# Attention block on one core: the small bias loads on SyncE's queue, the bias product behind the turning of the weight, and waits and orders around the images moved

## The reference

```python
residual = hidden_states                      # x: (16, 512, 32, 32) f32
h = group_norm(hidden_states, norm_gamma, norm_beta)   # 32 groups
q = conv1x1(h, wq, bq); k = conv1x1(h, wk, bk); v = conv1x1(h, wv, bv)
qf, kf, vf = (a.reshape(16, 512, 1024) for a in (q, k, v))
attn = softmax(einsum('bci,bcj->bij', qf, kf) * 512 ** -0.5, axis=2)
out = einsum('bcj,bij->bci', vf, attn).reshape(16, 512, 32, 32)
return residual + conv1x1(out, wo, bo)
```

## Time and profile before

| what | value |
|---|---|
| three runs | 2030.28, 2030.69, 2032.45 us, median 2030.69 |
| the profiled execution | 2031.8 us, its span in the trace 2029.9 us |
| instructions | 29828 |
| busy: PE, DVE, ACT, POOL | 98%, 80%, 49%, 16% of the span |
| mean granted clock of TensorE | 0.997 |
| HBM | 142 GB/s over the span |

### The profile page before, as it was taken

How to read it: one execution, slowest core, us unless ns; L and a number is a source line. 1 busy time by engine, 2 the same in 40 slices (tenths; PEclk the granted TensorE clock), 3 DMA queues, 4 the chain that set the end, 5 groups by cost and what they waited for, 6 DMA issues and landing times.

```text
span 2029.9 us, 29828 instructions
## 1 busy us (share of the span) xinstructions
PE 1985.6 (98%) x9924; PEld 1678.9 (83%) x9924; DVE 1630.4 (80%) x2284; ACT 999.5 (49%) x1529; POOL 325.8 (16%) x241
## 2 busy tenths in 40 slices
PE   9999999999999999999999999999999999999998
PEld 7787878878788787887878878787887878878887
DVE  7897787978879688696887969778797887978856
ACT  6464453645536464453644536445364553646443
POOL 2012120111202012020221201212011120201202
PEclk9999999999999999999999999999999999999999
DMA  6436152363424535154350533615236242363402
GB/s 238 150 146 162 60 163 93 145 165 124 102 84 151 159 145 124 42 176 134 145 155 31 174 116 145 159 74 150 93 145 165 98 119 93 146 164 145 86 28 42
DMA packets 55467, 255.45 MB, mean 126 GB/s; under 512 B 8208, under 2 KB 8208, under 8 KB 50832
## 3 DMA queue, kind: packets, MB, share of 16 engines
q1 hardware_dynamic: 34896, 221.53, 28.7%
q0 software_dynamic: 18432, 33.56, 11.1%
q10 hardware_dynamic: 2112, 0.01, 0.1%
HBM read 214.18 MB, written 74.45 MB: 142 GB/s over the span
## 4 chain that ended last, share of the span: by engine, by line
PE 81%; DVE 7%; DMA 7%; issue 3%; ACT 2%; POOL 0%; DVEq 0%; SPq 0%; POOLq 0%; ACTq 0%
PE psum L406 27%; PE psum L407 27%; PE psum L408 27%; DMA out<-scores 6%; DVE h_lo L955 3%; DVE scores L1186 1%; ACT scores L749 1%; DVE scores L1028 1%; DVE wide L1179 0%; DVE red L1174 0%; ACT scores L704 0%; DVE big_lo L1053 0%; DMA scores<-in_wq 0%; DVE bn L886 0%; DVE big_lo L1139 0%
## 5 line engine op out<-in xcount | busy, mean ns | idle before, releaser
L406 PE MATMUL psum<-big_hi 128*128 128x512 f32 x1056 | 411.9, 390 | 2.8 <-POOL big_lo L348 2.8
L407 PE MATMUL psum<-big_lo,big_hi 128*128 128x512 f32 x1056 | 411.9, 390 | 0.0
L408 PE MATMUL psum<-big_hi,big_lo 128*128 128x512 f32 x1056 | 411.5, 390 | 0.0
L406 PE MATMUL psum<-big_hi,h_hi 128*128 128x512 f32 x896 | 350.7, 391 | 3.9 <-ACT room L815 3.2
L407 PE MATMUL psum<-big_lo,h_hi 128*128 128x512 f32 x896 | 349.4, 390 | 0.0
L408 PE MATMUL psum<-big_hi,h_lo 128*128 128x512 f32 x896 | 349.3, 390 | 0.0
L1118 DVE TENSOR_TENSOR scores<-psum,room 128x512 f32<-128x512 f32 x192 | 130.7, 689 | 185.3 <-ACT room L815 135.3
L408 PE MATMUL psum<-w_split,h_lo 128*128 128x256 f32 x896 | 253.6, 283 | 0.0
L407 PE MATMUL psum<-w_split,h_hi 128*128 128x256 f32 x896 | 253.6, 283 | 0.0
L406 PE MATMUL psum<-w_split,h_hi 128*128 128x256 f32 x896 | 253.5, 283 | 0.0
L815 ACT COPY room<-psum 128x512 f32<-128x512 f32 x192 | 112.8, 587 | 275.5 <-PE psum L408 275.5
(11 more groups left out here) (133 smaller groups left out, 3448.2 us busy)
## 6 DMA issues: line engine op xcount, KB each, us to landing
w_split<-kept_t SPq DMA_DIRECT2D x15, 3584.0 KB, 11.8
w_split<-kept_v SPq DMA_DIRECT2D x15, 3584.0 KB, 11.3
room<-in_x SPq DMA_DIRECT2D x64, 512.0 KB, 3.4
out<-scores POOLq DMA_DIRECT2D x128, 256.0 KB, 6.8
room<-in_x SPq DMA_DIRECT2D x60, 256.0 KB, 4.7
red<-in_x SPq DMA_DIRECT2D x30, 256.0 KB, 4.6
wide<-in_x SPq DMA_DIRECT2D x30, 256.0 KB, 8.3
kept_t<-w_split SPq DMA_DIRECT2D x1, 3584.0 KB, 11.0
```

The costliest lines, as they stand in the source:

```text
L406: nc.tensor.matmul(o, a_hi, b_hi, start=start, stop=False, skip_group_check=True)
L407: nc.tensor.matmul(o, a_hi, b_lo, start=False, stop=False, skip_group_check=True)
L408: return nc.tensor.matmul(o, a_lo, b_hi, start=False, stop=stop, skip_group_check=True)
```

## The change

- The loads of bq, gamma, beta and bo go from ACT's queue to SP's: bq behind wk and wq and ahead of x, the other three behind wo and ahead of wv.
- On PE the four products with the bias (`bias_summed`) go behind the turning of wo; the copy of the result (`t_bias`) on ACT goes behind the first part of wv, and PE waits for it before the product of wo and wv.
- wo is no longer loaded again: the product of wo's rows with bv (`row_dots`) is made by DVE in `make_first_t` from the first copy of wo; bv's load comes early.
- In image 0 `high_wv(3..6)` and `low_wv(3..6)` go behind the first pair of scores, and the six pieces of statistics behind that pair's last sums.
- At each turn of images, DVE makes D3 of row 0 (`begin_t`) ahead of outputs 4 to 7, and waits for one store at a time (`left`), only ahead of the sum that overwrites it; ACT makes snap "b" and the high part of D3 ahead of the bias of outputs 4 to 6.
- In the last image the last output block gets its bias and x on DVE and is stored by a plain DMA of SP.

```diff
@@ scratch rows, semaphores
+        rest = room[:, 7, :]
-        wo_again = [scores[:, n, :] for n in (2, 3, 10, 11)]
-        bv_rows, wo_bv_terms = scores[:, 6, :], scores[:, 7, :]
+        bv_rows, wo_bv_terms = scores[:, 13, :], scores[:, 12, :]
...
@@ SyncE
                 sp.dma_start(wq_raw[:, o, :], w_d["q"][:, o, :]).then_inc(wq_in[o], 16)
+            sp.dma_start(bq_s[:], bq_d, allow_slow_non_contiguous=True).then_inc(bq_in, 16)
             for k in (2, 3, 0, 1):
                 sp.dma_start(full[:, k, :], x_d[0][:, k, :]).then_inc(x0_in[k], 16)
             for o in range(KC):
                 sp.dma_start(wo_raw[:, o, :], w_d["o"][:, o, :]).then_inc(wo_in[o], 16)
+            for n, a in enumerate(vec_d):
+                sp.dma_start(vecs[:, n, :], a, allow_slow_non_contiguous=True).then_inc(vec_in, 16)
             for o in range(KC):
                 sp.dma_start(wv_raw[:, o, :], w_d["v"][:, o, :]).then_inc(wv_in[o], 16)
+            sp.wait_ge(wv_split, KC)
+            sp.dma_start(bv_rows, bv.partition_broadcast(P)).then_inc(bv_in, 16)
...
-                    for c in range(KC):
-                        sp.dma_start(wo_again[c], w_d["o"][:, c, :]).then_inc(wo_back, 16)
-                    sp.dma_start(bv_rows, bv.partition_broadcast(P)).then_inc(bv_in, 16)
...
+                else:
+                    sp.wait_ge(h_split, count(b, 7, 7))
+                    sp.dma_start(rest, x_d[b][:, KC - 1, HALF:N]).then_inc(rest_held, 16)
+                    sp.wait_ge(rest_in, count(b, 16, 16))
+                    sp.wait_ge(last_added, 1)
+                    sp.dma_start(out_d[b, KC - 1, :, HALF:N], scaled(2 * KC - 1)).then_inc(last_stored, 16)
...
@@ GpSimd, the stores
-                for n in range(2 * KC):
+                for n in range(2 * KC if more else 2 * KC - 1):
@@ TensorE
-            pe.wait_ge(bias_step, 2)
-            for c in range(KC):
-                mm = nc.tensor.matmul(bank[7][:, c:c + 1], wide[:, 0, cols(c)], primer[:, 0:1],
-                                      start=True, stop=True, skip_group_check=True)
-            mm.then_inc(bias_summed, 1)
...
             for n in range(KC):
-                if n == KC - 1:
-                    pe.wait_ge(t_bias_set, 1)
                 for c in range(KC):
                     mm = nc.tensor.transpose(bank[KC + n][:, cols(c)], wo_raw[:, c, cols(n)], ident[:])
                 mm.then_inc(wo_turned, 1)
+            pe.wait_ge(wot_split, 1)
+            pe.wait_ge(bias_step, 2)
+            for c in range(KC):
+                mm = nc.tensor.matmul(bank[KC][:, c:c + 1], wide[:, 0, cols(c)], primer[:, 0:1],
+                                      start=True, stop=True, skip_group_check=True)
+            mm.then_inc(bias_summed, 1)
             for o in range(KC):
+                if o == 0:
+                    pe.wait_ge(t_bias_set, 1)
@@ ScalarE
-            act.dma_start(bq_s[:], bq_d, allow_slow_non_contiguous=True).then_inc(bq_in, 16)
-            for n, a in enumerate(vec_d):
-                act.dma_start(vecs[:, n, :], a, allow_slow_non_contiguous=True).then_inc(vec_in, 16)
...
                 nc.scalar.copy(wvs_hi[:, o, :], wv_raw[:, o, :]).then_inc(wv_high, 1)
+                if o == 0:
+                    act.wait_ge(bias_summed, 1)
+                    nc.scalar.copy(t_bias[:], bank[KC][:, 0:KC]).then_inc(t_bias_set, 1)
@@ ScalarE, later_parts
                         snap(b, r, 0, "a", T_AT[4])
-                        for n in (KC, KC + 1):
+                    snap(b, r, 1, "b", T_AT[2])
+                    high_t(b, r, "D3")
+                    if r == 0:
+                        for n in range(KC, 2 * KC - 1):
                             bias_output(b, n, last=True)
-                    snap(b, r, 1, "b", T_AT[2])
+                    snap(b, r, 2, "y", T_AT[6])
                     if r == 0:
-                        for n in (KC + 2, KC + 3):
-                            bias_output(b, n, last=True)
-                    high_t(b, r, "D3")
-                    snap(b, r, 2, "y", T_AT[6])
+                        bias_output(b, 2 * KC - 1, last=True)
@@ ScalarE, image
                             nc.scalar.copy(snap_s(q, n), bank[alpha_s[q % 2]][:]).then_inc(s_snapped, 1)
-                            if first and pair == 0 and n < 2:
-                                high_wv(3 + 2 * n + q)
...
+                    if first and pair == 0:
+                        for n in range(3, 7):
+                            high_wv(n)
@@ VectorE, first image
+            def row_dots(c):
+                if c:
+                    dve.wait_ge(bv_used, c)
+                nc.vector.tensor_tensor_reduce(out=wo_bv_terms, in0=wo_raw[:, c, :], in1=bv_rows, scale=1.0,
+                                               scalar=0.0, op0=ALU.mult, op1=ALU.add,
+                                               accum_out=wo_bv[:, c:c + 1]).then_inc(bv_used, 1)
             def make_first_t():
+                low_h(0, 1, True)
+                low_h(0, 2, True)
+                dve.wait_ge(bv_in, 16)
+                dve.wait_ge(vec_in, 16 * len(vec_d))
+                for c in (0, 1):
+                    row_dots(c)
+                low_h(0, 3, True)
+                sum_h(0, 2, True)
...
                 add_t(0, 1, "D3", True)
+                for c in (2, 3):
+                    row_dots(c)
+                dve.wait_ge(bv_used, KC)
+                nc.vector.tensor_tensor(out_bias[:], wo_bv[:], bo_s, ALU.add).then_inc(biases_set, 1)
@@ VectorE, make_t
+            def left(b, n):
+                dve.wait_ge(out_stored[n], count(b, 16, 0))
+            def begin_t(b):
+                left(b, 0)
+                add_t(b, 0, "D3")
             def make_t(b):
-                for n in range(KC):
-                    dve.wait_ge(out_stored[n], count(b, 16, 0))
-                add_t(b, 0, "D3")
                 low_t(b, 0, "D3")
+                left(b, 1)
                 add_t(b, 0, "D1")
+                left(b, 2)
                 add_t(b, 0, "D2")
+                left(b, 3)
                 add_t(b, 0, "B11")
...
-                for n in range(KC, 2 * KC):
-                    dve.wait_ge(out_stored[n], count(b, 16, 0))
                 add_t(b, 1, "D3")
...
                 add_t(b, 1, "D1")
+                left(b, 4)
                 add_t(b, 1, "D2")
+                left(b, 5)
                 add_t(b, 1, "B11")
+                left(b, 6)
                 add_t(b, 1, "B22")
+                left(b, 7)
                 add_t(b, 1, "B21")
@@ VectorE, first_weights and image
-                for n in range(7):
+                for n in range(3):
                     low_wv(n)
-            def first_bias():
...
                     if first and pair == 0:
-                        for n in range(6):
-                            next_piece(b, n)
+                        for n in range(3, 7):
+                            low_wv(n)
...
-                    for j in (q0, q1) if pair else (q1,):
-                        maximum(b, step, j)
-                        step += 1
+                    late = first and pair == 0
+                    if not late:
+                        for j in (q0, q1) if pair else (q1,):
+                            maximum(b, step, j)
+                            step += 1
...
+                    if late:
+                        for n in range(6):
+                            next_piece(b, n)
+                        dve.wait_ge(bn_set, PIECES + 6)
...
                 inverse(b, 1)
+                if more:
+                    begin_t(b + 1)
                 for n in range(KC, 2 * KC):
                     output(b, n)
+                if not more:
+                    dve.wait_ge(o_scaled, count(b, 8, 4 * KC))
+                    dve.wait_ge(rest_held, 16)
+                    nc.vector.scalar_tensor_tensor(scaled(2 * KC - 1), scaled(2 * KC - 1), out_bias[:, KC - 1:KC], rest,
+                                                   ALU.add, ALU.add).then_inc(last_added, 1)
```

41 lines of the change are left out of this document (11 added, 30 removed).

## The result

The changed kernel takes **1977.45 us** (median of 4 runs, 1976.81 to 1978.22) against 2030.49 for the kernel before on the same chip (4 runs, 2029.89 to 2032.45): a ratio of 0.9737 [0.972, 0.9754]. The profiled execution took 1976.81 us, its span is 1974.8.

A forecast was written before the change was run, and what follows sets the result against it. It took TensorE, busy 98% of the span, as the bound, so only its waits, start and end could be gained: 37.8 + 4.2 + 0.7 + 0.8 = 43.5 us, giving 1987 us, range 1983 to 2003.

The forecast's parts named there:

- Snap "b" and D3: At the 15 image turns: TensorE's waits for ACT's snap (8.9 us) and DVE's D3 (20.3 us) both go.
- 0.4 us to spare: At each turn: ACT's snap "y" ends at 294.1, and TensorE wants it for p = 3 at 294.6.
- 37.8 for the turns: Gain at the turns between images: 20.3 + 8.9 + 32 x 0.27 = 37.8 us.
- So each wait costs its idle plus 0.27: TensorE's listed waits at the turns: each loses its idle time and 0.27 us more in matmul spacing.
- just in time: At each turn: snap "a", waiting for DVE's last low_h, starts on ACT at 288.35, in time for p = 2.
- Image 0, net 4.2: First image: 5.2 us gained from the casts' wait and half clock, less 1.0 for lateness.
- The lateness of 1.0: Image 0: later low parts and statistics pieces carry through DVE to the first turn's snap "a"; bounds 0 and 2.5.
- The start, 0.7: Before the first images' scores: weights, x and statistics land earlier, gaining 0.7 us; bounds -0.5 and 1.3.
- rival E: At the start the clock stays at the 2.4 GHz level: 0.6 more, 1986 us; chance counted within the forecast's 0.63.
- The end, 0.8: After the last matmul: DVE add and plain SP store gain 0.2 of gap and 0 to 0.7 of landing.
- B: Rival: a new wait at each turn, snap "y" late behind three biases; 2008 us, or 1997 at half; chance 0.16.
- C: Rival: slower, D3 of row 0 held by store 0, landing L after 289.9, at each turn; 2039 us; chance 0.03.

The follow-up runs named there:

- a_loads_act: The changed kernel with the four small loads (bq, gamma, beta, bo) back on ACT's queue, the bias product staying behind the turning of wo: 1978.24 us, ratio 0.9744.
- the second: Profile of the changed kernel, unaltered, measured once more beside improved versions on one chip: 1977.60 us, ratio 0.9735; the profiled run took 1979.64.
- a_casts_old: The changed kernel with only the four casts high_wv(3) to high_wv(6) put back between ACT's first copies of the scores: 1981.58 us, ratio 0.9768.
- a_pieces_early: The changed kernel with image 0's six statistics pieces loaded after three low parts of v's weights (and the split of h), not seven: 1974.8 us, ratio 0.9737.

## Why the prediction was right and wrong

The direction and the mechanism at the turn were right; the size of the turn's term was not, and it took the time out of the range.

- **Snap "b" and D3: right.** Both waits are gone, as are D3's of row 0; each with the cause named (the two biases, the stores), since each comes back when its part is undone. "0.4 us to spare" for snap "y" is 0.45 in the trace (286.31 and 286.76).
- **37.8 for the turns: the step that failed.** "So each wait costs its idle plus 0.27" is right for the 32 waits of the list. The error was to take the list for all that TensorE loses at a turn. Measured: 48.0, so 10.2 were missing. Of these 4.1 lay at the first product of the scores (held by the low part of the late D3 of row 1), 1.5 at snap "a" and 1.6 in the half clock behind one long wait; another 1 was in waits for D3 of row 0 and snap "b" beyond the list, and the last 2 are spread in small differences. The period of the images, read from start to start in the trace of before, would have shown it: 124.19, while its 444 matmuls of 512 columns at 0.2267 and 168 of 256 columns at 0.12 fill 120.8.
- **Snap "a": wrong reason.** I had it "just in time" and counted it as neither loss nor gain. It was 0.10 late each turn, and became punctual because the small loads left ACT's queue (a_loads_act), which the prediction had costed at the start only.
- **Image 0, net 4.2: right within what one execution tells.** It gave 4.6 in the first profile and 2.9 in the second. The casts' wait and the half clock are worth 5.0 (125.85 in a_casts_old against 120.8 in a_pieces_early) where I had 5.2. The lateness of 1.0 (bounds 0 and 2.5) is 0.3 in the first profile and 1.7 in the second. Its cause is not DVE's own work, as I had it, but the landing of the pieces.
- **The start, 0.7: measured 0.0 in this pair of profiles.** Statistics begin at 12.05 against 12.15, because DVE has the weights 0.97 sooner and then waits 0.84 for x, ahead of which bq stands now. The first t product starts at 36.38 in both. Over more traces it starts at 36.3 to 36.9 with the four loads on ACT's queue (five) and at 34.1 to 37.5 with them on SP's and no fillers (ten), so 0.7 is neither confirmed nor excluded. What was wrong is the price of bq: I had it cost x some 0.5, and x lands 0.9 later for it here, 0.1 to 1.6 over the 13 traces. The Trainium skill, "DMA: Bandwidth & Descriptors", section Queues, rings and completion order, says that the descriptors of one issuing row are taken in ring order. The landings agree: x comes behind bq in every trace in which it was issued behind it.
- **The clock, rival E: did not come in the profiles of the changed kernel.** The bias product in the gap did not hold it up in nine of eleven traces; six matmuls of 512 columns did in four of four. Two traces of variants show what E would have been: there the first t product starts at 34.1 and 34.8.
- **The end, 0.8: measured 2.5.** The gap of 0.2 was right. The store lands 2.0 after issue in all 16 traces that have it, below my lower bound of 2.9 from loads, and the span ends 0.5 behind the landing instead of 1.2, a difference that the sum did not have. Here a load's landing on the same queue was no lower bound for a store's.
- **Rivals.** B (a late "y") and C (D3 held by a store) did not happen, and both were real: 28 and 46 us, each one edit away. C's point of decision, D3 about 2.6 late, has a measured neighbour: D3 is held 3.6 in the mean, where C's formula (L - 0.4 and 0.27) gives 3.5 a turn and 3.0 is measured. The kernel is then 7 us below the one before, not above, since image 0 and the end keep their gains and the turn had 3.3 to give where C had 2.5.

The sum with what was measured: 48.0 + 4.6 + 0.0 + 2.5 = 55.1, for 55.1 between the spans.
